# Scatters of a first attention issued singly, and in the tail each behind the last landing

## The reference

```python
x = x + _L0_xattn_ref(_layernorm(x), ctx_768, mask, Wq, Wkv)          # 16 heads of 8
x = x + _L0_ffn_ref(_layernorm(x), router_w, router_b, w1, b1, w2, b2)  # 8 experts, 2 per row, at most 1280 rows each
x = x + _L1_xattn_ref(_layernorm(x), ctx_768, w_q, w_k, w_v, w_out, b_out)  # 16 heads of 64
x = x + _L1_ffn_ref(_layernorm(x), w_router, gate_up_proj, ...)       # 16 experts, 1 per row, and a shared one
...
buf = jnp.zeros((E * cap + 1, d), x.dtype).at[slot].set(xf[st])       # in _L0_ffn_ref: rows sorted by expert
```

## Time and profile before

| what | value |
|---|---|
| median of 3 timed runs | 844.25 us (844.01 to 845.23) |
| span of the profiled execution, first to last instruction | 913.6 us |
| mean granted clock of PE in it | 0.968 of 2.4 GHz |
| busy: PE, DVE, ACT, POOL | 839.1, 600.8, 553.3, 474.1 us |
| scatters L806 on POOL | 64, 63.8 us busy, 996 ns each |
| DMA: packets, bytes | 84148, 87.37 MB |

### The profile page before, as it was taken

The page is one execution under the profiler, slowest core; times in us unless marked ns, Lnnn a source line. Parts: engine busy times, 40 slices in busy tenths (PEclk is TensorE's granted clock), DMA queues, the critical chain, the costliest instruction groups (busy, mean ns, idle before and its releaser), DMA issues.

```text
span 913.6 us, 31471 instructions
## 1 busy us (share of the span) xinstructions
PE 839.1 (92%) x11905; PEld 715.4 (78%) x11905; DVE 600.8 (66%) x1729; ACT 553.3 (61%) x1221; POOL 474.1 (52%) x575
## 2 busy tenths in 40 slices
PE   8998888878899998999999999999999998888786
PEld 3666555546589987998998998998999998867686
DVE  8886677734565647887777777677777676424343
ACT  4886676535387775776665666666666652225463
POOL 6333323463614436786656656655654444544455
PEclk9998999978799998999999999999999999999999
DMA  5455553513534432333553001001000002343330
GB/s 155 137 160 155 157 158 120 154 39 137 195 100 131 129 99 88 107 116 79 175 200 141 24 24 31 24 26 31 23 25 20 12 2 65 115 154 96 92 104 25
DMA packets 84148, 87.37 MB, mean 96 GB/s; under 512 B 15057, under 2 KB 70552, under 8 KB 83234
## 3 DMA queue, kind: packets, MB, share of 16 engines
q1 hardware_dynamic: 74946, 68.11, 24.7%
q0 software_dynamic: 8256, 17.01, 6.0%
q10 hardware_dynamic: 800, 0.24, 0.1%
HBM read 43.13 MB, written 40.44 MB: 91 GB/s over the span
## 4 chain that ended last, share of the span: by engine, by line
PE 81%; DVE 9%; issue 4%; ACT 2%; another core or an unknown queue 1%; DMA 1%; POOL 1%; SPq 0%; ACTq 0%; DVEq 0%; POOLq 0%
PE of L1367 8%; PE sf L1321 7%; PE jf L1242 6%; PE sf L1630 5%; PE sf L1283 4%; PE sf L1559 4%; PE mf L1269 4%; DVE cmx L2004 4%; PE jf L1251 3%; PE sf L1547 3%; PE sf L1458 3%; PE sf L1251 3%; PE of L1080 3%; PE sf L1033 2%; PE mf L1348 2%
## 5 line engine op out<-in xcount | busy, mean ns | idle before, releaser
L882 POOL TENSOR_TENSOR pl<-pT,ph 128x512 bf16<-128x512 f32 x128 | 146.1, 1165 | 105.1 <-DVE ph L2272 101.2
L806 POOL DMA_INDIRECT buf<-gu,slots x64 | 63.8, 996 | 88.9 <-PE of L1169 38.4
L2278 DVE TENSOR_REDUCE cmxb<-mf 128x8 bf16<-128x1024 f32 x64 | 78.2, 1222 | 43.6 <-PE mf L1348 39.2
L1700 ACT ACTIVATE pTf<-sf 128x1024 f32<-128x1024 f32 x64 | 62.6, 1022 | 36.6 <-PE sf L1040 18.0
L2004 DVE TENSOR_REDUCE cmx<-mf 128x8 bf16<-128x1024 f32 x64 | 78.1, 1220 | 10.0 <-PE mf L1061 6.8
L1818 ACT ACTIVATE pT<-sf 128x1024 f32<-128x1024 f32 x64 | 66.6, 1041 | 25.1 <-PE sf L1331 25.1
L1321 PE MATMUL sf<-qTs,kTs 64*128 64x128 f32 x1024 | 75.0, 286 | 1.6 <-ACT pT L1818 1.6
L871 POOL DMA_INDIRECT gb<-eo,slots x64 | 64.9, 1014 | 19.0 <-issue 18.9
L971 POOL DMA_INDIRECT out<-rows x47 | 46.3, 984 | 50.7 <-DVE rows L2677 39.7
L1321 PEld LDWEIGHTS sf<-qTs,kTs 64*128 64x128 f32 x1024 | 62.6, 188 | 7.1 <-issue 2.1
L1242 PE MATMUL jf<-wo,oT 128*128 128x128 f32 x496 | 62.9, 280 | 0.0
(11 more groups left out here) (353 smaller groups left out, 2725.4 us busy)
## 6 DMA issues: line engine op xcount, KB each, us to landing
buf<-zero SPq DMA_DIRECT2D x12, 516.0 KB, 7.1
rows<-buf SPq DMA_DIRECT2D x47, 129.0 KB
buf<-zero SPq DMA_DIRECT2D x22, 256.0 KB, 3.8
eo<-zero SPq DMA_DIRECT2D x22, 256.0 KB
ctxT<-in_ctxP SPq DMA_DIRECT2D x24, 192.0 KB, 2.4
rows<-buf SPq DMA_DIRECT2D x71, 64.0 KB
gu<-in_gu SPq DMA_DIRECT2D x4, 1024.0 KB
kept<-kTs SPq DMA_DIRECT2D x6, 512.0 KB
```

The costliest lines, as they stand in the source:

```text
L882: nc.gpsimd.tensor_tensor(pl[h][:, :, c, :], pT[h][:, :, c, :], ph[h][:, :, c, :], ALU.subtract)\
L2278: nc.vector.reduce_max(cmx1[b % 2][:, :].rearrange("p (r k) -> p r k", r=2)[:, :, 4 * h:4 * h + 4], M1p[:, :, :].rearrange("p r (c k) -> p ...
```

## The change

`scatters()` now takes one scatter of the queue ahead of adding new ones, under `plan[b, "scored"]`, and one after, under `plan[b, "weighed"]`. POOL issues the first behind a wait for the scores of batch b, the second behind a wait for the weighing of batch b-1. What is left at the end is nine scatters, not two. These nine, and the eight of round 6 behind `rstd_second(7)`, each stand behind a wait until all scatters sent before have landed. The eight of round 7 have no such wait.

```diff
     for b in STEPS:
+        plan[b, "scored"], queue = queue[:1], queue[1:]
         for r in rounds_at("rank", b - 1):
             queue += [(r, n, k) for n in round_batches(r) for k in range(2)]
-        some = 3 if b < NB - 2 else 4
-        plan[b], queue = queue[:some], queue[some:]
+        plan[b, "weighed"], queue = queue[:1], queue[1:]
     plan["end"] = queue
...
-                        if plan[b] and b in ENDING:
+                        for item in plan[b, "scored"]:
                             pool.wait_ge(sf_full, 4 * b + 4)
-                        elif plan[b] and b < NB:
+                            scatter_front(*item)
+                        for item in plan[b, "weighed"]:
                             pool.wait_ge(o_full, O_USE["pv", b - 1] + 1)
-                        for item in plan[b]:
                             scatter_front(*item)
+                    sent = 2 * NB - len(plan["end"]) - 4 * QH
                     for item in plan["end"]:
+                        pool.wait_ge(M0.scattered, 16 * sent)
                         scatter_front(*item)
+                        sent += 1
                     rstd_second(NQD - 1)
-                    for r in range(NQD - 2, NQD):
-                        for item in plan["end", r]:
-                            scatter_front(*item)
+                    for item in plan["end", NQD - 2]:
+                        pool.wait_ge(M0.scattered, 16 * sent)
+                        scatter_front(*item)
+                        sent += 1
+                    for item in plan["end", NQD - 1]:
+                        scatter_front(*item)
```

## The result

| | median of timed runs | ratio to before, 95% interval |
|---|---|---|
| before | 844.13 us (843.41 to 845.23) | |
| after | 880.51 us (880.07 to 881.02) | 1.043 (1.042 to 1.045) |

The change makes the kernel 36.4 us slower. The sign and the place were forecast, the size was not: 864 us, with a range that ended at 880. One later execution of the kernel before, on a chip where it otherwise takes 844 us, took 1101.6 us at a mean clock of 0.666; the ratios and the ranges given leave it out.

What follows compares the result with a forecast made beforehand. It took the kernel to be PE-bound, with the profile's stalls mostly absent from timed runs. Steps -2, later first expert tile +18.0, spills +2 and clock +2 made +20 us: 844.25 to 864 us, range 840 to 880.

Steps and rivals of the forecast that it cites:

- The stalls belong to the profiled execution: Stalls behind a third indirect transfer belong nearly all to the profiled execution; timed runs have at most a seventh of 82 us.
- the stalls are real: Rival: timed runs stall too, so the 19 steps gain 31 us and the kernel ends at 815 us; chance 0.14.
- Step 1: Steps 12 to 31 of the first attention: single scatters win 2 us, between nothing and at most 4.8 us.
- Never two within about 2 us: Steps 12 to 31: POOL's 39 single scatters would never go out two within about 2 us.
- Step 2: Tail backlog: nine scatters, not two, stand ahead of `rstd_second(7)`; its input is there at 207.5 us without stalls.
- Step 3: Tail: a serial scatter costs 2.25 us, landing 1.95 plus 0.30 between issues, where it was 1.27; bounds 1.95 and 3.4.
- step 5: Tail and early tiles: scatters meeting spills cost 2 us, PE's early tiles at the lower clock 2 us more.
- Step 4: Tail: `rstd_second(7)` begins 11.2 us later behind the ninth scatter, and the first expert tile starts 18.0 us later.
- the tail is worse: Rival: all 16 serial scatters of the tail cost 3.4 us, as beside steady spills, 881 us; no separate chance given.
- The nine waits themselves are nothing: Tail: the nine wait instructions ahead of `rstd_second(7)` add no cost of their own.

Runs made afterwards that it cites:

- before's second: Second trace of the kernel before, unchanged, on a chip where it runs in 844 us: profiled run 842.64 us, span 840.9 us.
- the waits by twos: The change with a landing wait before only every second of its seventeen waiting scatters: 865.93 us on an 844 chip, 905.73 and 908.08 us on 918 chips.

## Why the prediction was off

- **"The stalls belong to the profiled execution"**: false as a reason. On the 918 chips the timed runs are as slow as the traces with stalls (917.9 us), and on the 844 chips the profiled runs are as fast as the others (842.64 us by a span of 840.9). In all eighteen runs the profiled span is 1.6 to 1.8 us short of that execution's own time, and that time is at most 0.6% off the kernel's median. The rule of the Trainium skill (NOTIFIC — the notification-queue block, section 7.1) that I leaned on finds no support in them, though no run here is known to have gone without any trace. By every mark the front's trace is one of a 918 chip: a span of 913.6, a step 13 that goes on to 89.08 us (88.09 in a trace of a 918 chip, 83.53 in before's second), 659.4 us behind tile 0 (661 to 666 in the eight traces of the 918 chips, 625 to 629 in those of the others). That is inferred from those numbers; on which chip it was taken nothing shows.
- **What followed from it** held, and by luck: the timed runs came from an execution without stalls, and that was the case to sum. Leaving out 69 us as time that the *timed runs* do not have was right, and gave the right sign. The forecast that the profiled span would fall while the median rose also came true (913.6 to 878.4), but this test could not tell my reason from the right one: the trace of after was taken where there are no stalls, and on a 918 chip the change's span is 921.8 us. The rival "the stalls are real" (815 us) has its mechanism on the 918 chips, but not its time: there the steps get shorter by 17.6 us and the tail longer by more.
- **Step 1, the steps, -2 us**: measured -0.5, inside its bounds. "Never two within about 2 us" was wrong: behind an `rstd_second` both waits have long been met, and POOL issued at 85.36 and 86.75 us. The steps of 4.8 us that I expected are 5.3: those without scatters in the trace were no measure of all. The share left to the timed run, 12.6 of 82, was a little over the seventh that the bound of 4.8 us took.
- **Step 2, the input of the last rows at +10.6 us behind step 31's start**: +12.0. The last single scatter came at 177.86, +3.3, where I had +0.6, since `values(30)` ends later without a stall than I took. That is 2.6 us of error in after; before's own tile 0 came 2.8 us later too (+40.15 against +37.4), so the two cancel.
- **Step 3, "I take 2.25" for a serial scatter, is the term that was mis-sized.** It measured 3.02 us undisturbed, which makes 16 x 0.77 = 12.3 us of the 17.5 by which the spans (37.5) exceed the sum (20). The rest is 2.5 us of longer intervals, 1.2 us of clock (both in step 5) and 1.5 us of step 1. Two parts make up the 0.77: 0.3 us between landing and next issue was taken from two issues without a wait, where a wait on a DMA's semaphore leaves 0.8 (2.23 to 3.02 above); and the transfer, seen done at 1.95 from its bytes, was signalled at 2.23. The second had been in the page: the Trainium skill (DMA: Bandwidth & Descriptors, section "Anatomy of one DMA — SWDGE (gpsimd) path") gave an estimate of 2.15, which the trace's 2.23 supports. With the same gap of 0.3 the estimate was 2.45 a piece, and still 0.57 short. The gathers' 3.1 us, which I had kept as the far end, was the nearest row for the whole interval, though by chance: it is the time from issue to landing alone.
- **Step 4, the chain**: right in kind. `rstd_second(7)` follows the ninth scatter, PE waits for the last rows (23.3 us, not 10), and tile 0 waits for the scatters. From the last scatter's issue to tile 0 it took 4.9 us, where I had 5.1.
- **Step 5, the extras**: four intervals of 3.6 to 4.35 us are 4.2 us above the others, where I had 2. Each of them had spills beside it (DMA share 1.02 in one, 0.06 in an undisturbed interval), as step 5 has it; a run without spills was not made. The clock: 3.2 us behind tile 0, where I had 2; from 249.5 to 255 us it stood at 0.50. That the lower clock also slows PE's keys and values in the tail was not costed. In the change the scatters cover it; in the version without waits, where the last keys came 8.4 us later behind an `rstd_second(7)` only 3.8 us later, they do not.
- **The rival "the tail is worse", 881 us**, met the measured time to the microsecond, in part by luck: it took 3.4 us a scatter where 3.3 was measured, and left out its own -2 and the 2 us of clock. Its condition, spills beside every scatter, was not what made the price: 12 of the 16 intervals, 3.01 to 3.23 us, were near the price without it. It was argued away by the DMA engines' busy share (0.41), which is no measure of a latency: after's tail has 0.30.
- **"The nine waits themselves are nothing"**: each left 0.8 us between landing and issue where I had 0.3.

Nothing that ran beats both kernels on both kinds of chip. On the 918 chips the waits by twos do, by 1.2 to 1.4%, and lose 2.6% on the others.

## What to carry to other kernels

A wait for a DMA's landing in a serial chain cost a nearly fixed time each (here 3.0 us from issue to issue where issues alone go at 1.27); price it from a row in which an engine was released by a DMA, never from when the bytes moved. Such waits cost less when they let two go at a time (866 against 880 us), and they should stand where nobody on the critical path queues behind them. An operation that others wait for, here `rstd_second(7)`, would go ahead of the backlog; that order was not tried. If the profile's span and the timed median disagree by 8%, say first that they may come from two machines, and ask for a second trace before reading any stall as real or as made by the profiler.

## What was not expected of the hardware

- Two of the five chips ran this kernel in 918 us and three in 844 (ratio 1.087): medians of 13 to 23 runs 917.9 and 917.6 (single ones 908.4 to 924.1), and 843.95, 843.2 and 843.8. On the slower ones ACT got a result of PE late behind nine scatters in a row (idle 11.7 us by "remote"), and with a landing wait before every second one much less so (3.2 us); the steps took 124.5 us with threes and 106.9 with single scatters. From which number in a row the stall begins was not tried. The last stretch, from 530 us behind tile 0 to the end and untouched by the change, takes 134.8 us there and 98.4 on the others. Why the chips differ no run here shows.
- Even with single scatters steps 12 to 30 are slower there, 106.9 us against 101.3.
- PE's clock fell to 1.2 GHz after a wait of 5.0 us in the version without waits, and stayed there for 13.7 us of nearly full work (13.56 of 13.70 us busy).
